# Places of the attention matrix, the packed keys and queries, and the state in one fused layer kernel

## The reference

```python
xn = _layernorm(x)
# attention: chunked scan over the tokens, K = 64, Di = 512
x_ = xn @ up_w.T; shift = silu(causal_conv(x_)); q, k = shift @ q_w.T, shift @ k_w.T
v = sigmoid(x_ @ ig_w1.T @ ig_w2.T + ig_b2) * x_
o_inter = einsum('bck,bkv->bcv', qt * exp(b), S)
A = einsum('bik,bjk,bijk->bij', qt, kt, D)
o = o_inter + einsum('bij,bjv->biv', A, vt)
S = exp(btot)[:, :, None] * S + einsum('bck,bcv->bkv', k_dec, vt)
o = rmsnorm((o + shift * residual_weight) * silu(xn @ gate_w.T)) @ down_w.T
# feed-forward: 256 -> 1024 -> 1024 -> 1024 -> 256
h = silu(w1(xn)) * w2(xn); h = gelu(h1(h)); h = gelu(h2(h)); return x + o + w3(h)
```

## Time and profile before

| | us |
|---|---|
| median of 3 runs | 1938.95 (1938.8 to 1940.89) |
| the profiled execution | 1940.21 |
| its span | 1938.4 |
| TensorE matmuls busy | 1921.8 (99%) |
| TensorE weight loads busy | 1902.9 (98%) |
| VectorE busy | 1584.1 (82%) |
| ScalarE busy | 1295.3 (67%) |
| GpSimd busy | 81.2 (4%) |

### The profile page before, as it was taken

How to read it: one execution, slowest core, us unless ns; L and a number is a source line. 1 busy time by engine, 2 the same in 40 slices (tenths; PEclk the granted TensorE clock), 3 DMA queues, 4 the chain that set the end, 5 groups by cost and what they waited for, 6 DMA issues and landing times.

```text
span 1938.4 us, 46120 instructions
## 1 busy us (share of the span) xinstructions
PE 1921.8 (99%) x16804; PEld 1902.9 (98%) x16804; DVE 1584.1 (82%) x4304; ACT 1295.3 (67%) x2687; POOL 81.2 (4%) x136
## 2 busy tenths in 40 slices
PE   8999999999999999999999999999999999999998
PEld 7999999999999999999999999999999999999998
DVE  7788888888788887888888788787888878888887
ACT  5666667767676766666766667675667666667575
POOL 0000000000000000000000000000000000000000
PEclk9999999999999999999999999999999999999999
DMA  8000000000000000000000000000000000000000
GB/s 309 7 12 13 12 2 12 12 12 12 13 1 12 13 12 12 8 5 13 12 13 12 7 6 12 13 12 13 1 12 13 12 12 12 1 13 12 13 7 8
DMA packets 23538, 34.19 MB, mean 18 GB/s; under 512 B 3170, under 2 KB 19810, under 8 KB 23364
## 3 DMA queue, kind: packets, MB, share of 16 engines
q1 hardware_dynamic: 23364, 31.43, 4.8%
HBM read 23.04 MB, written 8.39 MB: 16 GB/s over the span
## 4 chain that ended last, share of the span: by engine, by line
PE 94%; issue 2%; ACT 1%; DVE 1%; SPq 1%; DMA 0%; POOLq 0%; POOL 0%; DVEq 0%; ACTq 0%
PE fb L383 64%; PE ab L383 21%; PE ab L593 2%; PE ab L628 1%; PE ab L529 1%; PE ab L453 1%; PE ab L518 1%; PE ab L583 1%; PE fb L678 1%; SPq L289 0%; PE ab L590 0%; PE ab L469 0%; PE ab L606 0%; ACT wwhole L726 0%; DMA sgate<-stage_w 0%
## 5 line engine op out<-in xcount | busy, mean ns | idle before, releaser
L383 PE MATMUL fb<-hid1h,wwhole 128*128 128x256 f32 x2048 | 474.2, 279 | 0.1
L383 PE MATMUL fb<-hid1l,wwhole 128*128 128x256 f32 x2048 | 467.9, 276 | 0.0
L383 PE MATMUL fb<-hid0l,wwhole 128*128 128x256 f32 x2048 | 465.9, 276 | 0.0
L383 PE MATMUL fb<-hid0h,wwhole 128*128 128x256 f32 x2048 | 465.8, 276 | 0.0
L383 PEld LDWEIGHTS fb<-hid1h,wwhole 128*128 128x128 f32 x2048 | 384.5, 188 | 4.0 <-ACT raw L838 0.3
L383 PEld LDWEIGHTS fb<-hid1l,wwhole 128*128 128x128 f32 x2048 | 384.7, 188 | 0.0
L383 PEld LDWEIGHTS fb<-hid0h,wwhole 128*128 128x128 f32 x2048 | 384.5, 188 | 0.0
L383 PEld LDWEIGHTS fb<-hid0l,wwhole 128*128 128x128 f32 x2048 | 384.4, 188 | 0.0
L838 ACT ACTIVATE raw<-fb,sh_s 128x256 f32<-128x256 f32 x512 | 212.3, 465 | 150.3 <-PE fb L383 142.7
L383 PE MATMUL fb<-xntl,wwhole 128*128 128x256 f32 x1024 | 237.5, 276 | 0.0
L383 PE MATMUL fb<-xnth,wwhole 128*128 128x256 f32 x1024 | 237.5, 276 | 0.0
(11 more groups left out here) (234 smaller groups left out, 4481.6 us busy)
## 6 DMA issues: line engine op xcount, KB each, us to landing
xin<-x SPq DMA_DIRECT2D x32, 256.0 KB, 2.7
out<-xin SPq DMA_DIRECT2D x32, 256.0 KB, 2.2
stage_more<-stage_w SPq DMA_DIRECT2D x6, 512.0 KB, 7.1
sgate<-stage_w SPq DMA_DIRECT2D x4, 512.0 KB, 4.4
shift<-stage_w SPq DMA_DIRECT2D x4, 512.0 KB, 5.0
v<-stage_w SPq DMA_DIRECT2D x4, 512.0 KB, 5.6
raw<-stage_w SPq DMA_DIRECT2D x3, 512.0 KB, 6.0
mixed<-stage_w SPq DMA_DIRECT2D x3, 512.0 KB, 8.2
```

What stands on the lines that cost most here:

```text
L383: mm = pe.matmul(o, a, b, start=start and i == 0, stop=stop and i == len(pairs) - 1)
```

## The change

It allocates kdq ahead of the state tiles and adds two gaps: atth, attl and kdq start at 384 and stateh and statel at 448 bytes modulo 512, counted from wwhole's start. The small tiles behind them move by 256 bytes. Nothing else differs.

```diff
         att = sb("att", [P, NC, CH])
+        lie_off(6)
         atth, attl = sb("atth", [P, 2, CH], F32R), sb("attl", [P, 2, CH], F32R)
+        kdq = sb("kdq", [P, N], F32R)
+        lie_off(7)
         stateh, statel = sb("stateh", [P, DI], F32R), sb("statel", [P, DI], F32R)
-        kdq = sb("kdq", [P, N], F32R)
         kd, qhl = kdq[:].rearrange("p (c a k) -> p c a k", c=NC, a=2), kdq[:]
```

## The result

| | before | after |
|---|---|---|
| median, us | 1940.89 (5 runs, 1938.80 to 1942.35) | 1949.73 (5 runs, 1949.12 to 1950.19) |
| the profiled execution, us | 1940.21 | 1949.73 |
| its span, us | 1938.4 | 1947.9 |

The ratio is 1.0047, with a 95% interval from 1.0036 to 1.0058: the change makes the kernel slower by 8.8 us, where 3.5 us faster was forecast, from the 1938.95 of the first three runs of before. In after the lines behind the new ones are two higher (the helper `wide` is L385, the outputs' last matmuls L630).

The account below looks back on a forecast made before the run. TensorE's matmul steps were taken as the only bound; outputs 3.2 less entry 0.3 plus state update 0.6 gave 3.5 us off, from 1938.95 to 1935.45 us, with an eight-in-ten range of 1933.8 to 1939.0.

Parts of the forecast that it names:

- nothing but the steps counts: TensorE matmuls: as the only bound, each nanosecond off a step comes off the span.
- everything else at the same steps: Expected trace of after: stages outside outputs and state update keep their steps, with no new wait on TensorE.
- D: Output matmuls: new places cost 0.0067 us each, 3.4 us, plus 0.1 at the state update; 1942.45 us; chance 0.07.
- The last list of the prediction: Signs of being wrong: outputs stay at 283 ns, halves don't shorten, or hid loops change though their tiles don't move.
- The contradiction that I set aside: Data at 448 over weights at 0: slow in warm-up, quick in main loops; the loops were taken as nearer witness.
- rows 7: Warm-up blocks of 14 equal matmuls at different places, read as steps of 0.113 or 0.118 to 0.120 us.
- (1) Outputs: Output matmuls at 0.1134 us: second half 2.27, saving 0.13; first half 1.36, saving 0.07; 3.2 us over sixteen sequences.
- rival B: Outputs take the 0.1177 step, saving 1.2 us, and the state update 0.3; 1937.45 us; chance 0.17.
- (2) Entry: First steps of the outputs may stay slow: 0.01 us a half, 0.3 us lost in all, between 0 and 0.6.
- (3) State update: Four 512-column matmuls go from 0.230 to 0.220 us each, saving 0.04 us, 0.6 in all; bounds 0 and 1.1.
- (4) The rest: Moved k_sq, read by one transpose in each of 32 halves: at most 0.2 us either way, taken as 0.
- The rule: TensorE reads moving data and weights through independent ports, so places could not matter; time would stay, 1938.95 us.

Follow-up runs that it names:

- e4: After with atth, attl and kdq at 0 instead of 384, so output matmuls stream 64 bytes (modulo 512) from the weights loaded beneath: 1961.26 us, ratio 1.0108.
- e3: Before with only the small tiles behind kdq moved, by 256 bytes: 1939.71 us, ratio 0.9994.
- e2: After with only the state moved to 448; atth, attl and kdq at 192 as in before: 1940.49 us, ratio 0.9999.
- e1: After with only atth, attl and kdq moved to 384; state and small tiles at their old places modulo 512: 1953.49 us, ratio 1.0070.
- e5: After plus one matmul of 16 moving columns ahead of the last block of h2 in each second half: 1951.12 us, ratio 1.0056.
- e7: e4 plus one matmul of 16 moving columns ahead of the last block of h2 in each second half: 1952.83 us, ratio 1.0058.
- e8: After plus one matmul of 256 moving columns ahead of the last block of h2 in each second half: 1949.74 us, ratio 1.0048.
- e6: Before plus one matmul of 16 moving columns ahead of the last block of h2 in each second half: 1946.87 us, ratio 1.0029.
- e9: After with half of the second input-gate matmul done once more ahead of it, in first halves only: 1945.65 us, ratio 1.0030.
- e10: After with the projection's parth matmuls first and the wait for partl only ahead of the partl ones, none added: 1944.39 us, ratio 1.0020.
- e11: Before with the projection order and later partl wait of e10: 1939.82 us, ratio 0.9992.

## Why the prediction was wrong, point by point

**The bound** was right: TensorE's steps alone make the time, and everything that was lost is steps at full clock with no wait ahead of them.

**The step that failed** is the sentence that "nothing but the steps counts", read as the steps of the matmuls whose tiles move. I priced 512 output matmuls and 64 of the state update and took the other 16,000 as fixed by their places. They are not: their step has two lasting values. In second halves the outputs' new length or end made it the slow one behind them (0.38 us in 15 halves, 5.7 in all). In first halves the start of the projection decides it (five with h1 at 15.08, 4.9 us and 0.5 more in the projection); how the change reaches that start isn't shown. The prediction had all this under "everything else at the same steps", priced at nothing. Nothing in my four rivals let the change act on a stretch that it doesn't touch, so that even the slower rival (D, 1942.45) had the wrong place and well under half of the size. The last list of the prediction did name the sign, that the hid loops change though their tiles don't move; it was given no price.

**The contradiction that I set aside** was the evidence. Data at 448 over weights at 0 took 1.81 us in a warm-up block and the quick step in the loops. I called the loops the nearer witness; by what the runs showed it was more likely one pair of places in both rhythms, though no run tried the warm-up blocks again. That weakens the whole reading of rows 7 as a table of good and bad distances. The last half of before, shown above, said the same.

**(1) Outputs.** Of two steps the size was wrong. The second half's took 2.36 us, not 2.27 (0.1180 a step, rival B's 0.1177), first halves gained 0.02 and not 0.07. That 0.1134 was possible is shown by e4, with distance 64, and in second halves alone.

**(2) Entry.** I allowed 0.01 us a half for the way into the outputs. The way out was not considered at all; it cost 0.38 us in a second half.

**(3) State update**, forecast at 0.88 us for four, down from 0.92. In the timeline of after

```profile
97.89 0.39 PE L606 MATMUL ab<-parth,kdq 128*128 128x512 f32 x1
98.11 0.62 PE L608 MATMUL ab<-partl,kdq 128*64 128x512 f32 x2
98.58 0.39 PE L609 MATMUL ab<-parth,kdq 128*128 128x512 f32 x1
```

the first to the third start takes 0.69 us, as before; the gain is at most some 0.01 us where 0.04 was forecast.

**(4) The rest** was right: e3 moves the small tiles alone and shows nothing.

**The rule** that loading the next weights takes no read bandwidth from the running matmul (the Trainium skill, TensorE: Matmul & The Clock Gate, "Step-by-step: what each phase is for") would, as I read it, have given no change. What I drew from it, that the place can't matter, isn't borne out: the same 20 matmuls take 2.40, 2.36 and 2.27 us in before, after and e4, which differ in places alone. Whether the weights' read is what slows them no run shows; 2.36 and 2.27 are 0.118 and 0.113 a step, the two rhythms again, and these occur with the same places too. Its no change was all the same nearer to what was measured than my forecast.

**What stays open.** Why one entry leads to one rhythm and one to the other isn't shown, nor why h1's slow rhythm goes on into h2 in after and not in e2. A matmul of 16 columns ahead switched it in 15 second halves and not in the last half. It is also open why slow first halves are more frequent with atth at 384 or 0 (5 to 13 of 16 in after, e1, e4, e5, e7 and e8) than at 192 (0 or 1 of 16 in before, e2, e3 and e6). No matmul between the loop's turn and the projection reads a moved tile. e9 and e10 show that the first halves with h1 at 15.08 hang on the projection's entry, as with another entry there are none; that the outputs' length shifts TensorE against VectorE by a fraction of a ns, differently in each sequence, is my guess and was not tried.

## What to carry to other kernels

Where TensorE is the only bound, a stretch of matmuls can be slowed by what stands ahead of it, so list the stages by count and length for every repeat, also the last, before pricing an edit: two lengths for the same stage are the warning, and then an edit's own saving is no forecast of the time. A local gain is to be tried with the stretches behind it in view, and with another entry (one small matmul, another order) before the place itself is judged. In the changed kernel, a wait that was met only just in time went with two lengths of what follows; waiting for that operand later (e10) removed the slow one, and in before (e11) it cost nothing in the median. A shorter stage can also come back as a longer step elsewhere, as at the loop's turn in e5 and e8.

## What the runs showed of the hardware

With 128x128 weights loaded for each 256 columns at the full clock the steady step is 113.3 ns or about 117.7 ns (7.27 against 7.54 us for 64, 14.51 against 15.08 for 128), and 120.0 for the outputs of before. A stream keeps its step for 88 to over 220 matmuls; in after, e1, e4, e5, e7 and e8 the slow one went from h1 through the score matmuls into h2 each time (15.08 and then 11.50 or 11.51 us), in e2 it ended there (15.08, then 11.10). Every first stretch behind the norm's sum is quick in all kernels (3.63 us for its 32 matmuls of w1 and w2). One matmul of 16 columns ahead of a stretch, which delays it by 0.11 us, switched it in both directions, in 15 of 15 second halves each, and in neither kernel in the last half.
